# A graph-transformer layer on one core: three pieces of TensorE's work placed behind the key/value or mixing work of the same third of a group

## What is computed

```python
xn = layernorm(x)
m  = xn[src] @ W[:256] + edge @ W[256:]
h  = segment_sum(m * norm[dst], dst) + h_bias        # norm = 1/sqrt(degree)
k, v = ln(xn @ w_k + b), ln(xn @ w_v + b)            # per head, 8 heads of 32
kv   = sum over nodes of k^T v / 6250
mix  = gelu((q @ kv + xn) @ w1 + b1) @ w2 + b2 + xn
x2   = x + h + mix
out  = x2 + layernorm(ffn(layernorm(x2)) + layernorm(x2))   # ffn: the 2 experts chosen from the mean row
```

## Time and profile before

| | |
|---|---|
| median of 3 runs | 1610.23 us (1606.24 to 1611.78) |
| profiled execution, from its first to its last instruction | 1630.3 us (the only time of it that is given) |
| busy, share of that span | PE 72%, PEld 49%, DVE 40%, ACT 34%, POOL 56% |
| granted TensorE clock, mean | 0.872 of full speed |
| 110 to 690 us | edges with the key/value work |
| 690 to 760 us | edges with the folding of weights |
| 760 to 1255 us | edges with the mixing work |
| 1345 to 1630 us | dense part |

### The profile page before, as it was taken

How to read it: one execution, slowest core, us unless ns; L and a number is a source line. 1 busy time by engine, 2 the same in 40 slices (tenths; PEclk the granted TensorE clock), 3 DMA queues, 4 the chain that set the end, 5 groups by cost and what they waited for, 6 DMA issues and landing times.

```text
span 1630.3 us, 22836 instructions
## 1 busy us (share of the span) xinstructions
PE 1173.3 (72%) x7416; PEld 803.1 (49%) x7416; DVE 654.6 (40%) x1698; ACT 559.7 (34%) x1157; POOL 915.7 (56%) x975
## 2 busy tenths in 40 slices
PE   0157767776686777766676767677776839999997
PEld 0033333433343343334445444453554539999997
DVE  5633223323223333221233244243432446676775
ACT  4731111111111111111333343333342457677674
POOL 6166666666666666666666666666666103344342
PEclk9988987888788888778798897889898959999999
DMA  9976666656665666486677787777777341222221
GB/s 234 319 216 202 181 194 185 205 177 180 201 193 174 189 199 181 127 260 204 206 225 232 220 240 248 225 223 241 234 225 238 103 136 40 71 61 76 64 68 39
DMA packets 209235, 295.03 MB, mean 181 GB/s; under 512 B 20940, under 2 KB 180146, under 8 KB 207887
## 3 DMA queue, kind: packets, MB, share of 16 engines
q1 hardware_dynamic: 152899, 165.66, 34.7%
q0 software_dynamic: 39888, 108.97, 22.1%
q10 hardware_dynamic: 16350, 19.20, 3.5%
HBM read 261.75 MB, written 32.00 MB: 180 GB/s over the span
## 4 chain that ended last, share of the span: by engine, by line
another core or an unknown queue 31%; PE 30%; issue 14%; DVE 9%; ACT 9%; DVEq 2%; DMA 2%; SPq 2%; ACTq 1%; POOL 0%; POOLq 0%
PE bank L1156 8%; PE bank L1167 8%; PE bank L944 2%; PE bank L997 2%; PE bank L938 2%; DVEq L1324 2%; PE bank L930 2%; PE bank L1003 1%; ACT fl L649 1%; PE bank L1041 1%; ACT L751 1%; ACT L731 1%; DVE acc L1326 1%; DVE xc L1339 1%
## 5 line engine op out<-in xcount | busy, mean ns | idle before, releaser
L583 POOL DMA_INDIRECT ring<-xn_table,src_sb x807 | 781.8, 969 | 465.7 <-issue 221.1
L930 PE MATMUL bank<-ring,s 128*32 128x512 f32 x1662 | 283.6, 667 | 65.3 <-DVE s L1298 42.6
L944 PE MATMUL bank<-fl_t,wg 128*128 128x128 f32 x1120 | 158.7, 300 | 51.6 <-ACT fl_t L649 36.7
L944 PEld LDWEIGHTS bank<-fl_t,wg 128*128 128x128 f32 x1120 | 146.7, 211 | 54.8 <-ACT fl_t L649 38.8
L938 PE MATMUL bank<-ident,fl 128*128 128x128 f32 x280 | 60.9, 356 | 146.9 <-ACT fl L649 131.7
L1326 DVE TENSOR_TENSOR acc<-acc,bank 128x96 f32 x277 | 70.7, 255 | 226.5 <-issue 87.4
L938 PEld LDWEIGHTS bank<-ident,fl 128*128 128x128 f32 x280 | 39.3, 177 | 222.2 <-ACT fl L649 170.7
L1331 DVE TENSOR_TENSOR xt_lo<-bank,xt_hi 128x250 fp32r<-128x250 f32 (+1 forms) x75 | 37.9, 505 | 260.7 <-ACT xt_hi L649 173.0
L649 ACT ACTIVATE xt_hi<-bank 128x250 fp32r<-128x250 f32 (+1 forms) x75 | 33.4, 446 | 285.6 <-remote 227.3
L712 ACT ACTIVATE kvn<-xc 125x512 f32<-125x512 f32 x50 | 31.5, 630 | 262.1 <-DVE xc L1339 135.3
L1156 PE MATMUL bank<-xf_hi,fw_hi 128*128 128x256 f32 x400 | 113.5, 284 | 9.4 <-DVE fw_lo L1628 7.2
(11 more groups left out here) (221 smaller groups left out, 2374.1 us busy)
## 6 DMA issues: line engine op xcount, KB each, us to landing
ring<-edges SPq DMA_DIRECT2D x207, 512.0 KB
ring<-xn_table,src_sb POOLq DMA_INDIRECT x807
xnr<-xn_table SPq DMA_DIRECT2D x50, 125.0 KB
xnr<-xn_table SPq DMA_DIRECT2D x25, 250.0 KB
xch<-x SPq DMA_DIRECT2D x25, 250.0 KB
base_rows<-xch ACTq DMA_DIRECT2D x25, 250.0 KB
x_rows<-xch ACTq DMA_DIRECT2D x25, 250.0 KB
xt_cols<-xte ACTq DMA_DIRECT2D x25, 250.0 KB
```

What stands on the lines that cost most here:

```text
L583: pool.indirect_dma_start(out=to, out_offset=None, in_=rows, in_offset=bass.IndirectOffsetOnAxis(ap=index, axis=0),).then_inc(done, 16)
L930: mm = pe.matmul(ps_seg[t % 2][j * W:(j + 1) * W, :], lhsT=s32[:, t % 3, j * TS + i, :].bitcast(F32), rhs=ring[:, u, j, :], start=i == 0, ...
L944: mm = pe.matmul(ps_y[:, o * P:(o + 1) * P], lhsT=wg[:, c, o * P:(o + 1) * P], rhs=fl_t[:, c, :], start=c == 0, stop=c == 3)
```

## The change

PE calls `transposes` in the thirds i=0, and `columns_free`, `node_columns` and `project` in the thirds i=1. They stood right behind `strip_sums`; now they stand behind whatever key/value, folding or mixing work the same third has. Their waits move with them. `turn_rows` keeps its place at the end of the thirds i=2. The other engines' queues are the same, and no instruction is added or removed.

```diff
                 if q < NQ:
                     strip_sums(q)
-                if i == 0 and 1 <= t <= NG:
-                    transposes(t - 1)
-                if i == 1 and t:
-                    columns_free(t)
-                    if fin_at(t, 0) is not None:
-                        pe.wait_ge(s_acc, min(strips_before(DONE[fin_at(t, 0)]), NS))
-                        node_columns(fin_at(t, 0))
-                if i == 1 and 1 <= t <= NG:
-                    if t == 1:
-                        pe.wait_ge(s_par, 16 * 11)
-                    project(t - 1)
                 if kv_at(q, 5) is not None:
                     accumulate(kv_at(q, 5))
...
                 if mix_at(q, 1) is not None:
                     mix_first(mix_at(q, 1))
+                if i == 0 and 1 <= t <= NG:
+                    transposes(t - 1)
+                if i == 1 and t:
+                    columns_free(t)
+                    if fin_at(t, 0) is not None:
+                        pe.wait_ge(s_acc, min(strips_before(DONE[fin_at(t, 0)]), NS))
+                        node_columns(fin_at(t, 0))
+                if i == 1 and 1 <= t <= NG:
+                    if t == 1:
+                        pe.wait_ge(s_par, 16 * 11)
+                    project(t - 1)
                 if i == 2 and fin_at(t, 2) is not None:
                     turn_rows(fin_at(t, 2), mixes_turned(q))
```

## The result

The changed kernel took 1615.97 us (median of 18 runs, 1612.62 to 1622.66), the kernel before, timed beside it, 1612.01 us (18 runs, 1606.24 to 1616.45). The ratio as recorded is 1.0031 with an interval of [1.0021, 1.0042] (the two medians alone give 1.0025): a little slower, where 25 us less were forecast. The profiled execution is a run of 1619.33 us, 3.4 us above the median, with a span of 1617.5 us; of the one of before, on which the forecast rests, only the span is known, 1630.3 us, 18 us above this second median. The ratios in this document compare runs in the faster of two states of the chip, which leaves out only two of the six runs of one kernel (the one before with VectorE's additions moved), its profiled run among them.

A forecast was written before the change was run, and what follows sets the result against it. The prediction took POOL's gathers, delayed by ring slots PE had not yet signalled free, to bound the edge stages. Gains of 5.8 us (key/value) and 20 us (mixing), about 25 us, from 1610.2 us gave 1585 us, range 1545 to 1632 us.

The forecast's parts named there:

- The bound: Both edge stages advance at POOL's pace, busy 65% in each; back to back, four gathers make a third 5.0 us.
- The moves in the waits: Edge stages: ACT's 119.8 us for `mix_first` fall well, T's wait falls about 3 us, K's wait replaces T's in thirds i=0.
- the slower rival: Key/value stage: P starts 3.0 us later, delaying DVE's additions and `xt_lo`; 44 us lost, 1654 or 1629 us; chance 0.24.
- the second term of the sum: Mixing stage: of 30.5 us that POOL waits for slots PE releases late, two thirds, 20 us, are gained.
- The rival "none": Edge stages: the release hangs on POOL falling idle, whatever PE's order; 1610 us, a few us either way; chance 0.20.
- the chain's gain of 2.9 us: Mixing stage: with `mix_first` signalled before P, ACT's gelus run during the wait and T starts up to 2.9 us earlier.
- The first term: Key/value stage: all of PE's lateness in POOL's six waits with L930 as releaser goes, 5.8 us gained.
- Late signals as unchanged: Both edge stages: 116 us of POOL's waits for late signals, cause unknown, counted as no gain.
- The rule that weight loads measure PE's load: Key/value stage: PE has 60% of its time free, so its order alone is worth nothing unless another engine waits for it.

The follow-up runs named there:

- the changed kernel with late additions: The changed kernel with VectorE's additions of P's product moved from third i=2 to the end of the next third i=0: 1633.5 us, ratio 1.0114.
- `mix_second` behind: The changed kernel with `mix_second` put behind T, the node columns and P again: 1627.87 us, ratio 1.0001 to the kernel before.
- both halves' profiles: Profiles of the kernel before with only T moved (ratio 0.9996) and with only the node columns and P moved (ratio 1.0092).
- T's half: The kernel before with only the transposes T (thirds i=0) moved behind the key/value or mixing work: 1613.08 us, ratio 0.9996.
- P's half: The kernel before with only the node columns and P (thirds i=1) moved behind the key/value or mixing work: 1629.47 us, ratio 1.0092.
- The pair on one chip: The changed kernel with `mix_second` behind T, columns and P again (1.0001), and the kernel before with `mix_first` alone ahead of them (1.0102).
- plain loads and the new order: The changed kernel with the edge stages' gathers, all but the first six slots, replaced by plain loads of the same bytes: 1347.02 us, ratio 0.9138.

## Why the prediction was wrong

- **The bound was right for the key/value stage.** It advances at the pace of the gathers, 5.0 us for a third at least (5.06 measured on the prompt chip), and without them it took 367.4 us instead of 469.9. For the mixing stage the prediction took the same bound from GpSimd's equal 65%. There the best order on a late chip comes to the gathers' 5.8 us, but on the prompt chip the stage took 499.2 us with the gathers and 516.0 us without, so they don't set its pace there.
- **The moves in the waits were right in kind.** ScalarE's wait for `mix_first` fell from 119.8 to 28.1 us, T's waits for `fl` from 52.4 to 4.7 us in the key/value stage, and K's wait took their place, 64.3 to 83.5 us. The additions wait for P as the slower rival described (202.8 us, 4.3 before), but that rival's 44 us did not follow: the changed kernel with late additions had 66 us less of K's wait, and the pace was the same.
- **The step that failed** is the second term of the sum: "Mixing stage: 34.7 - 14 x 0.3 = 30.5 us in 14 waits, 2.2 us each, against 2.9 us that the chain gains; I take two thirds, 20 us". It took a wait whose releaser is PE as time that an earlier S gives back. Measured, these waits did not fall to about 10 us but rose to 40.6 us. With `mix_second` behind they did fall, and then an S that ends earlier is only released remotely: 34.7 became 25.0 and 53.5 became 60.9 us, and the ratio is 1.0001. The rival "none", to which the prediction gave 0.20, is what came. Its condition ("ACT's and PE's waits move as described, but POOL still takes 5.9 us for a third") was met, at 5.80 us, and the same 138 or 139 gathers stand in both halves' profiles. Its cause, a release that hangs on GpSimd falling idle, was not tested. The longest remote wait of GpSimd's is 2.2 to 3.0 us in both stages of every profile with four gathers on a late chip, whatever the order, which would fit it.
- **A second part of that step**: the chain's gain of 2.9 us counted `mix_first` but not that `mix_second` would now wait in front of T and P, 32.6 us in 11 waits, for `hm_lo` behind late additions. Without it (the kernel with `mix_second` behind) the ratio is 1.0001. That the 0.3% is its price is not shown, and the two halves speak against it: T's half has 46.7 us of this wait in 15 times and a ratio of 0.9996, P's half 15.7 us and 1.0092. By the table the 0.3% would lie in the mixing stage (544.7 us, T's half 541.0), as far as single profiles tell; its cause stays open.
- **The first term**, 5.8 us in the key/value stage, failed in the same way. The waits for L930 went, and 82.3 us of remote ones stay; T's half, whose time is that of the kernel before, has 83.1 us together. The pair on one chip shows the exchange: 8.9 us less for L930, 8.9 us more remote, and 565.3 against 564.9 us for the stage. That the profile before had 91.2 goes with its long span: it lay 18 us above its median, and I priced waits from it without a second profile.
- **Late signals as unchanged** was right in the sum, taking them as nothing gained, and their cause could be narrowed: they stayed with every order of PE tried, and went with the gathers or with another chip.
- **The rule that weight loads measure PE's load** (the Trainium skill, Perfetto Trace Analysis, Identifying the Most-Contended Engine), by which PE's order alone is worth nothing, would have given the right answer: PEld was busy 81.76 of 200 us. With plain loads and the new order PEld is still only 102.44 of 200 us, and there the order is worth 2.0%, so the rule's reason isn't what decided.

## What to carry to other kernels

In these runs a wait on a released buffer was refilled by another one as soon as it was shortened. It can be won back only if the buffer's next user isn't itself at its floor: take the pacing engine's work away (here plain loads for gathers) and see what the change is worth without it, before pricing any wait. Do so stage by stage: here two stages with the same busy share of GpSimd had different limits. When several engines wait on each other, price a move by what it puts at the head of a queue in front of others, not only by what it lets through. And take two profiles of the kernel before, on more than one chip if possible: here one chip ran the kernel in 8.6% less time than the others (1473.9 against 1613.06 us), more than any edit of the order.

## What the runs showed of the hardware

The same kernel took 1474 us on one chip and 1612 to 1629 us on others, with gathers of the same 967 to 969 ns each. One late chip took 1613.84 us in one comparison and 1629.11 us in a later one, so the time at which a kernel runs counts as well. Between 300 and 500 us a gather comes every 1.44 to 1.48 us on the late chips instead of every 1.27 us, whether a slot has three or four, and signals of PE reach other engines microseconds behind the end of the matmul in the records, 6.5 us in the earlier trace rows. Neither is seen with the prompt chip, where the same signal took 0.03 us, nor are late signals on a late chip with plain loads. The Trainium skill (Perfetto Trace Analysis, DMA Instruction — SWDGE (GPSIMD)) says that the record of such a gather ends when its descriptors are written, not when the data are moved. The rows agree as far as they go: the record is the same 0.97 us on both kinds of chip, while the pace differs; they don't show the data's movement itself. Which part of a gather holds the signals up, its descriptors or its transfers of single rows, was not tried, and what sets the chips apart stays open.
